# Next batch's key and query fills behind all part writes, an earlier normalisation in one unit, another buffer for the last rows

## What is computed

```python
xn = layernorm(x)
# attention layer; DH = 128, 8 heads of 16
x1 = layernorm(xn[..., :DH] + mha(xn[..., :DH], branch 1)) * g1 + be1
xs = holt(xn)                       # a linear recurrence along the tokens
x2 = layernorm(xs[..., :DH] + mha(xs[..., :DH], branch 2)) * g2 + be2
y  = concat(x1, x2)
a  = layernorm(y + relu(y @ w_ff1.T + b_ff1) @ w_ff2.T + b_ff2) * g_ff + be_ff
f  = relu(xn @ W1 + b1) @ W2 + b2    # the second net
out = x + a + f
```

## Time and profile before

| What | Value |
| --- | --- |
| Median of the runs shown | 2667.15 us |
| The profiled execution, its own time | 2665.81 us |
| Its span, first to last instruction | 2664.3 us |
| TensorE busy | 2508.3 us, 94% |
| ScalarE busy | 2189.6 us, 82% |
| VectorE busy | 1511.9 us, 57% |
| GpSimd busy | 339.9 us, 13% |
| Mean granted TensorE clock, as a share of full speed | 0.973 |
| Moved by DMA | 95.94 MB, mean 36 GB/s |

### The profile page before, as it was taken

One profiled execution on the slowest core, in us unless ns is written; L12 is line 12 of the kernel. 1 busy time (PEld: TensorE's weight loads), 2 busy tenths in 40 slices (PEclk: granted clock), 3 DMA queues, 4 the chain that ended last, 5 costly groups with the idle time before them and its releaser, 6 DMA issues.

```text
span 2664.3 us, 68736 instructions
## 1 busy us (share of the span) xinstructions
PE 2508.3 (94%) x30081; PEld 995.9 (37%) x30081; DVE 1511.9 (57%) x3206; ACT 2189.6 (82%) x2419; POOL 339.9 (13%) x317
## 2 busy tenths in 40 slices
PE   6999999987999999999799999998979999999896
PEld 4233333344633333324463333332545333333254
DVE  5345555564754555565475455556547545555667
ACT  5899999963599999996459999998646999999863
POOL 1101100012411010011340101001044010100142
PEclk9999999998999999998899999999989999999998
DMA  8102100006111010000511201000141020100001
GB/s 218 66 10 42 27 16 10 6 6 122 48 57 26 17 34 10 10 6 21 106 48 57 34 10 34 10 10 6 45 82 48 26 34 10 34 10 10 6 22 48
DMA packets 49683, 95.94 MB, mean 36 GB/s; under 512 B 7888, under 2 KB 32464, under 8 KB 48992
## 3 DMA queue, kind: packets, MB, share of 16 engines
q1 hardware_dynamic: 41440, 72.07, 9.7%
q0 software_dynamic: 7936, 19.41, 4.9%
HBM read 57.31 MB, written 34.08 MB: 34 GB/s over the span
## 4 chain that ended last, share of the span: by engine, by line
PE 83%; DVE 9%; DMA 4%; ACT 2%; issue 1%; POOL 1%; DVEq 0%; SPq 0%; ACTq 0%; POOLq 0%
PE slot L1443 33%; PE slot L1417 19%; PE slot L1205 16%; PE slot L1492 5%; PE slot L1476 5%; DMA part_dram<-p_sb 3%; PE slot L1325 1%; POOL p_sb L578 1%; DVE hid_parts L865 1%; DVE o_sb L818 1%; DVE rs L749 1%; DVE hid_one L861 1%; PE slot L1272 1%; DVE hid_parts L863 1%; DVE p_sb L987 1%
## 5 line engine op out<-in xcount | busy, mean ns | idle before, releaser
L700 ACT ACTIVATE p_sb<-slot 128x1024 f32<-128x1024 f32 x2048 | 1911.4, 1031 | 139.4 <-PE slot L1417 132.5
L1443 PE MATMUL slot<-p_sb,v_sb 128*17 128x512 f32 x8192 | 1075.7, 599 | 31.3 <-DVE o_sb L818 24.7
L1417 PE MATMUL slot<-q_st,k_st 50*128 50x512 f16 x4096 | 623.9, 383 | 5.5 <-ACT p_sb L700 3.1
L1417 PEld LDWEIGHTS slot<-q_st,k_st 50*128 50x128 f16 x4096 | 117.2, 94 | 881.4 <-ACT p_sb L700 870.7
L861 DVE TENSOR_SCALAR hid_one<-slot,b_grown 128x256 f32<-128x256 f32 x256 | 123.9, 484 | 266.5 <-PE slot L1205 264.7
L1443 PEld LDWEIGHTS slot<-p_sb,v_sb 128*17 128x17 f32 x8192 | 181.5, 97 | 244.1 <-ACT p_sb L700 185.1
L873 DVE SCALAR_TENSOR_TENSOR second<-slot,second 128x256 f32<-128x256 f32 x64 | 27.2, 425 | 385.1 <-PE slot L1205 385.1
L1205 PE MATMUL slot<-w_parts,hid_parts 128*32 128x256 f16 x6144 | 216.2, 275 | 13.4 <-DVE hid_one L861 13.4
L827 DVE RECIPROCAL rden<-den 128x256 f32<-128x256 f32 x128 | 224.3, 1753 | 7.8 <-DVE hid_parts L865 0.5
L1476 PE MATMUL slot<-area,wf_parts 128*128 128x512 f16 x768 | 176.1, 390 | 53.7 <-ACT p_sb L716 51.4
L1205 PE MATMUL slot<-xt_parts,w_parts 128*32 128x256 f16 x6144 | 214.8, 274 | 4.1 <-DVE hid_one L861 4.1
(11 more groups left out here) (111 smaller groups left out, 1783.9 us busy)
## 6 DMA issues: line engine op xcount, KB each, us to landing
part_dram<-p_sb SPq DMA_DIRECT2D x16, 1024.0 KB, 8.4
xn<-x SPq DMA_DIRECT2D x16, 512.0 KB, 7.0
second<-x SPq DMA_DIRECT2D x32, 256.0 KB, 3.1
ffn_dram<-second SPq DMA_DIRECT2D x32, 256.0 KB, 2.0
area<-ffn_dram SPq DMA_DIRECT2D x16, 512.0 KB, 5.2
out<-area SPq DMA_DIRECT2D x15, 512.0 KB, 3.3
k_st<-part_dram SPq DMA_DIRECT2D x24, 256.0 KB, 10.5
q_st<-part_dram POOLq DMA_DIRECT2D x24, 256.0 KB, 19.8
```

Of the source, the lines that this page charges most:

```text
L700: act.activation(p_sb[:, n % 4, :], slot[n % 3][:, :], ACT.Exp, scale=0.25 / GROW ** 2).then_inc(exp_done, 1)
L1417: mm = pe.matmul(slot[at % 3][:, k * CHUNK:(k + 1) * CHUNK], k_st[rows_, pair, kt * P:(kt + 1) * P], q_st[rows_, pair, c_ * CHUNK:(c_ + 1) ...
L1443: mm = pe.matmul(o_bank[ROW * j:ROW * j + DK + 1, :], v_sb[:, a, kt, GH * g + j, :], p_sb[:, n % 4, (j % 2) * CHUNK:(j % 2 + 1) * CHUNK], ...
```

## The change

- `fill` of `k_st` for batches 1 to 3 leaves the middle of SyncE's prologue. With the `q_st` fill and `fill_max`, which leave GpSimd's program for these batches, it makes `next_stacks`, issued by SyncE in `results` behind all four part writes and behind the load of `x4` for chunk 0. `max_out(b, 1)` follows it. The query fills of batches 1 to 3 have a semaphore of their own, `q_next_in`. Batch 0 stays as it was.
- In unit 14 `y_stats` stands between portions 4 and 5, `rsqrt` and `y_normalised` between 5 and 6, `check_sums` between 6 and 7.
- The last chunk of the last batch is made in `xn` and not in `o4`, and its `finish` doesn't wait for `stored`.

```diff
                 def prologue(b):
                     part_out(b, 0, 0)
                     part_out(b, 0, 1)
-
-                    hold(sp, k_out, 16 * 2 * b + 16 + 16)
-                    fill(sp, 0, ALL_PAIRS, k_st, K_PART, 0, k_first_in)
+                    if b == 0:
+
+                        hold(sp, k_out, 16 + 16)
+                        fill(sp, 0, ALL_PAIRS, k_st, K_PART, 0, k_first_in)
                     max_out(b, 0)
                     part_out(b, 1, 0)
                     part_out(b, 1, 1)
+                    if b == 0:
+                        max_out(b, 1)
+
+                def next_stacks(b):
+
+                    hold(sp, k_out, 16 * 2 * b + 16 + 16)
+                    fill(sp, 0, ALL_PAIRS, k_st, K_PART, 0, k_first_in)
+                    hold(sp, q_out, 16 * 2 * b + 16 + 16)
+                    fill(sp, 0, ALL_PAIRS, q_st, Q_PART, 1, q_next_in)
+                    hold(sp, m_out, 16 * (2 * b + 1))
+                    fill_max(sp, 0, ALL_PAIRS, q_next_in)
                     max_out(b, 1)
...
                         sp.dma_start(x4, one(ffn_dram, b, cc)).then_inc(back_in, 16)
-                        tiles = slice(0, CT)
-                        if halves and cc == CHUNKS - 1:
+                        if cc == 0 and not final:
+                            next_stacks(b + 1)
+                        if final and cc == CHUNKS - 1:
                             hold(sp, o_half_ready, 1)
-                            sp.dma_start(one(out_v, b, cc)[:, 0:CT // 2, :], o4[:, 0:CT // 2, :]).then_inc(stored, 16)
-                            tiles = slice(CT // 2, CT)
-                        hold(sp, o_ready, n + 2)
-                        sp.dma_start(one(out_v, b, cc)[:, tiles, :], o4[:, tiles, :]).then_inc(stored, 16)
+                            sp.dma_start(one(out_v, b, cc)[:, 0:CT // 2, :], xn[:, 0:CT // 2, :]).then_inc(stored, 16)
+                            hold(sp, o_ready, n + 2)
+                            sp.dma_start(one(out_v, b, cc)[:, CT // 2:CT, :], xn[:, CT // 2:CT, :]).then_inc(stored, 16)
+                        else:
+                            hold(sp, o_ready, n + 2)
+                            sp.dma_start(one(out_v, b, cc), o4).then_inc(stored, 16)
...
                 def middle(b):
                     refill(b)
                     for cc in range(CHUNKS - 1):
                         first_y(b, cc)
-                    prologue(b + 1)
                     nets(b)
                     residual(b + 1)
...
-                    dve.wait_ge(stored, 16 * (n + 1))
+                    if halves == 1:
+                        dve.wait_ge(stored, 16 * (n + 1))
                     dve.wait_ge(y_ready, n + 2)
+                    o_all = o4 if halves == 1 else xn[:, 0:CT, :]
                     for h in range(halves):
                         tiles = slice(h * CT // halves, (h + 1) * CT // halves)
-                        o_part = o4[:, tiles, :]
+                        o_part = o_all[:, tiles, :]
...
                             hidden_half(b, i, 4)
-                            if n > 0:
+                            if n == UNITS2 - 2:
+                                y_stats(b, 1)
+                            elif n > 0:
                                 check_sums(b, n - 1)
                             hidden_half(b, i, 5)
                             if n == UNITS2 - 2:
-                                y_stats(b, 1)
+                                rsqrt(2 * CT)
+                                y_normalised(b, 1)
                             hidden_half(b, i, 6)
                             if n == UNITS2 - 2:
-                                rsqrt(2 * CT)
-                                y_normalised(b, 1)
+                                check_sums(b, n - 1)
                             hidden_half(b, i, 7)
...
                                 hold(pe, k_first_in, 16 * K_LOADS * (b + 1))
-                                hold(pe, q_first_in, 16 * Q_LOADS * (b + 1))
+                                if b == 0:
+                                    hold(pe, q_first_in, 16 * Q_LOADS)
+                                else:
+                                    hold(pe, q_next_in, 16 * Q_LOADS * b)
```

More of the change, by code:

```diff
@@ L372, in fast_programs @@
             q_first_in = sem("q_first_in")
+            q_next_in = sem("q_next_in")
             xt_rounded = sem("xt_rounded")
@@ L490, in attention, with results @@
                             load_half(b, i + 2)
-                def results(b, halves=False):
+                def results(b):
+                    final = b == B - 1
                     hold(sp, second_out, 16 * (HALVES * (b + 1) + 2))
@@ L515, in last @@
                     hold(sp, pv_done, TILES * UNITS2 * (b + 1) + 2)
-                    results(b, True)
+                    results(b)
                 sp.sem_inc(stored, 16)
@@ L540, in spilled, with first_stacks @@
                     hold(pool, m_out, 16 * (br + 1))
-                def prologue(b):
+                def first_stacks(b):
                     hold(pool, q_out, 16 * (2 * b + 1) + 16)
@@ L582, in first @@
                 def first(b):
-                    prologue(b)
+                    first_stacks(b)
                     pool.wait_ge(wf_split, 2)
@@ L920, in finish @@
                         step.settle()
-                        normalise([o4[:, t, :] for t in range(tiles.start, tiles.stop)])
+                        normalise([o_all[:, t, :] for t in range(tiles.start, tiles.stop)])
                         step(dve.tensor_tensor(o_part, o_part, rows("gamma_ff", CT // halves), ALU.mult))
```

## The result

The changed kernel takes 2604.59 us, median of 4 runs (2603.17 to 2612.27), against 2667.6 us before (4 runs, 2662.42 to 2673.88). The ratio is 0.9769, with a 95% interval from 0.974 to 0.9797. The forecast was 2602, its range 2592 to 2618. The profiled execution took 2603.41 us, its span 2601.9; before it was 2665.81 and 2664.3.

The account below looks back on a forecast made before the run. At a passage between batches the bound was taken to be the landing of branch 1's query part behind fills. Gains of 58.8 + 1.6 + 3.0 = 63.4 us off 2665.81 gave 2602.4, stated as 2602, range 2592 to 2618.

Parts of the forecast that it names:

- The landing: Batch passages: branch 1's last query part lands in 5.1 us, hidden behind TensorE's first block; 58.8 us gained over three passages.
- (a): Passages: query part lands at the opening's 10.4 us, ScalarE starts 4.3 us later each; 2615 us, chance 0.10.
- (d): Passages: ScalarE's wait stays because the part shares with whatever is in flight; 2667 us, chance 0.02.
- (e): Passages: wait stays and fills on one queue run at half rate, part lands 29 us later; 2748 us, chance 0.03.
- What comes late next: Passages, after the wait goes: first maxima, VectorE's normalisation beside GpSimd and the moved fills cost nothing.
- rival (b): Passages: fills on one queue are slower and chunk 0's store waits, about 5 us each; 2618 us, chance 0.05.
- Unit 14: Reordered VectorE work saves 0.4 us of idle time a batch, 1.6 us in all, range -8 to 15.
- rival (c): Unit 14's meeting comes out otherwise: 2589 us without the block, 2612 with TensorE's pause counted; chance 0.08.
- The step that speaks of the meeting: Unit 14: GpSimd's two scalings block VectorE's cast and subtraction 3.8 us; order only moves this to portion 6, gaining nothing.
- TensorE's new pause ahead of portion 7: Unit 14: TensorE makes portion 7 some 2 us later than it wants to; costed at nothing.
- The last rows: Last chunk: without the wait for chunk 2's store its first half starts 3.0 us sooner; gain 3.0, at least 2.
- The sum: Whole run: 58.8 + 1.6 + 3.0 = 63.4 us off the profiled 2665.81, giving 2602.4, stated as 2602.

Follow-up runs that it names:

- e1: Kernel before with only the fills moved, unit 14 and the last rows as before: 2615.86 us, median of 4, ratio 0.9786.
- e4: The changed kernel as it is, run again: 2601.76 us, median of 4, ratio 0.9738.
- e12: The changed kernel with 72 already satisfied waits at the end of GpSimd's program: span 2604.6 us, one run.
- e5: The changed kernel with query fills of batches 1 to 3 on GpSimd's queue, issued behind the part writes: span 2589.4 us, one run.
- e6: The changed kernel with all fills of batches 1 to 3 on SyncE ahead of branch 1's part writes: 2664.38 us, one run.
- e7: The changed kernel with key fills of batches 1 to 3 ahead of branch 1's part writes, query fills behind: span 2624.9 us, one run.
- e9: The changed kernel with GpSimd scaling y's second chunk only after unit 14's rows are attended: 2587.11 us, median of 4, ratio 0.9702.
- e3: Kernel before with only the last chunk's rows made in another buffer, xn: 2664.93 us, one run.
- e2: Kernel before with only unit 14's new order: span 2657.4 us, one run.
- e11: e9 with unit 13's check_sums moved behind unit 14's eviction and query fills on GpSimd behind all part writes: 2573.09 us, median of 5, ratio 0.9627.

## Why the prediction was right, and where it was lucky

**The landing.** Issue to landing 5.1 us was taken from branch 0's part; 5.0 to 5.1 was measured. ScalarE's start, 1.55 us behind TensorE's first product, was forecast at 1.5. The nets' stretches gave 59.25 us for 58.8, and e1, e4 and e12 repeat it to 0.1 us. Rivals (a), (d) and (e) fall by the landing. This is the mechanism that was forecast, and e5, e6 and e7 bear it out; here the prediction wasn't lucky.

**What comes late next.** Nothing, as forecast: the three nets' stretches of the changed kernel are 123.30 us each. The first maxima land in 1.6 us for 22.6, and VectorE's normalisation beside GpSimd's line 595 moved nothing that these stretches show. The fills took their 27 us and were done some 10 us before chunk 0's store; rival (b) falls.

**Unit 14.** 0.4 us a batch forecast, 0.41 to 0.43 measured, and rival (c) falls on both its sides. The step that speaks of the meeting was the one worth having, and it was used only to say that the edit gains nothing there. It held the larger gain: 15 us with one wait added. The sum has no term for unit 15, and there it was incomplete: the idle time that TensorE has in unit 14 is paid a second time in unit 15 by the clock, 8.4 us in e9's comparison and, less surely, 2.4 with the new order. TensorE's new pause ahead of portion 7 cost nothing in the stretch, as said.

**The last rows.** Forecast 3.0, measured 3.15 in e3 against either profile of before. In the first pair of profiles the stretch shows only 1.45. There the last batch's first chunk ran its first products at half clock (12.21 us for line 1499's 48, 10.53 before), which took the rest. The same half clock there, and 1.6 to 1.9 us with it, is in five more of the 14 profiles (e1, e2, e9, e11, e12), with and without this edit.

**The sum.** 63.4 us forecast, 62.4 between the two profiled executions, 63.0 between the medians. That the total came so close is in part luck: 6.1 us of tail were lost that no step had named, 6.2 us of clock in the passages were won by the draw of two executions, and 1.7 lost the same way in the last chunk. e4, with the same code, lost those 6.2 and more in its passages and still had the better median, 2601.76. The last step also slipped: the profiled execution lies 1.3 us below the median, so 2602.4 for it means about 2603.7 for the median, and 2602 was given. The range of 2592 to 2618 names the spread between executions and so covers the draws; nothing in its reasons covers the tail.

## What to carry to other kernels

Look at what is in flight ahead of the transfer that an engine waits for, not at its own size: here 1 MB took 26 us behind 3 MB of small-row fills and 5 us in front of them, on either queue. Where TensorE pauses because another engine is full, count the pauses twice, once as they stand and once for TensorE's clock behind them (here 15.1 us in unit 14 and some 6 in unit 15, over four batches). A stretch that the trace shows blocked by another engine's instruction is won by moving that other instruction, not by reordering the blocked one.

## What the runs showed of the hardware that I had not expected

- The last stretch of a run depends on the code. GpSimd's `DRAIN` at the end took 2.43 or 3.08 us where GpSimd issues the query fills and 9.94 us where SyncE does, and the tail was 5.2 to 5.5 us against 11.5 to 11.6, in all 14 profiles. The cause is open.
- TensorE's granted clock fell to half while its record showed no idle time, for some 7 us at a cost of 3.1 us (14 times) or some 10 us at a cost of 4.7 us (4 times), in 18 of 42 passages, each time at the same place, by the same eight products of 38 and 2 rows. Two profiles of one kernel can differ by more than 6 us by this, which is more than two of the three edits here give. Stretches between fixed instructions, compared over several profiles, told 0.4 us apart where medians couldn't tell 3.
- Fills with rows of 4 KB into 16 partitions moved at about 120 GB/s and 1 MB writes at about 400, in the profiles read here (before, after, e7); with all fills on SyncE the rate was the same as with both queues.
